# Full-height adapter products in a gated state-space and mixture-of-experts block

## The reference, cut to what matters

```python
xe   = x + w @ muW.T
gate = silu(fused(xe, gW, gqa, gqb, gs, w))
up   =      fused(xe, uW, uqa, uqb, us, w)
out  = fused(gate * up, dW, dqa, dqb, ds, w)

def fused(x, W, qa, qb, scale, w):          # 352 inner features, 8 adapters of rank 8
    a   = einsum('th,krh->tkr', x, qa)      # 64 values a token
    b   = einsum('tkr,khr->tkh', a, qb)
    return x @ W.T + scale * einsum('tkh,tk->th', b, w)
```

## Time and profile before

| what | value |
|---|---|
| median of three runs | 1694.26 us |
| fastest, slowest run | 1688.27, 1695.64 us |
| span of the profiled execution | 1685.8 us |
| PE busy | 1568.4 us, 93% |
| DVE busy | 1155.5 us, 69% |
| POOL busy | 737.8 us, 44% |
| ACT busy | 617.2 us, 37% |
| granted PE clock, mean | 0.977 |

### The profile page before, as it was taken

One profiled execution on the slowest core, in us unless ns is written; L12 is line 12 of the kernel. 1 busy time (PEld: TensorE's weight loads), 2 busy tenths in 40 slices (PEclk: granted clock), 3 DMA queues, 4 the chain that ended last, 5 costly groups with the idle time before them and its releaser, 6 DMA issues.

```text
span 1685.8 us, 19547 instructions
## 1 busy us (share of the span) xinstructions
PE 1568.4 (93%) x6856; PEld 1155.1 (69%) x6856; DVE 1155.5 (69%) x1634; ACT 617.2 (37%) x971; POOL 737.8 (44%) x537
## 2 busy tenths in 40 slices
PE   3787799798888999999999999999999999999999
PEld 2343377566666677777777777777777777777776
DVE  5798964788999867487888755778888553333333
ACT  5545443444454434443343244333433321111111
POOL 4488510489898801077777301376786000000000
PEclk8799999899999999999999999999999999999999
DMA  7688627688787664765667445587665456566552
GB/s 251 215 285 315 254 80 253 201 290 297 270 289 286 253 255 172 248 228 205 232 238 258 152 161 196 202 275 257 238 208 180 175 200 210 184 222 222 195 181 85
DMA packets 111473, 375.87 MB, mean 223 GB/s; under 512 B 20176, under 2 KB 45776, under 8 KB 94864
## 3 DMA queue, kind: packets, MB, share of 16 engines
q1 hardware_dynamic: 101904, 340.81, 57.8%
q10 hardware_dynamic: 9472, 33.82, 5.8%
HBM read 304.33 MB, written 70.25 MB: 222 GB/s over the span
## 4 chain that ended last, share of the span: by engine, by line
PE 63%; DVE 18%; issue 5%; ACT 5%; POOL 4%; DMA 3%; SPq 0%; ACTq 0%; DVEq 0%; POOLq 0%
PE b_g L735 14%; PE b_u L735 14%; PE b_u L826 7%; DVE ring L1493 4%; PE b_g L826 3%; PE b_q L781 3%; PE b_q L826 3%; PE b_g L799 2%; DVE ring L1499 2%; PE b_g L766 2%; DVE tt L1467 2%; POOL ring L1392 2%; PE b_g L759 1%; POOL yx L1401 1%; DVE z L1467 1%
## 5 line engine op out<-in xcount | busy, mean ns | idle before, releaser
L1392 POOL TENSOR_TENSOR ring<-du,rep 128x512 f32<-128x512 f32 x256 | 344.5, 1349 | 151.4 <-DVE du L1571 91.9
L735 PE MATMUL b_g<-xnb,gm 128*128 128x512 f32 (+1 forms) x1440 | 356.2, 396 | 0.9 <-DVE xnb L1470 0.9
L735 PE MATMUL b_u<-xnb,gm 128*128 128x512 f32 (+1 forms) x1440 | 349.1, 391 | 0.0
L1493 DVE TENSOR_TENSOR_SCAN ring<-b_a,ring 128x512 f32<-128x512 f32 x256 | 310.8, 1214 | 15.7 <-ACT b_a L964 8.4
L1401 POOL TENSOR_TENSOR yx<-yx,ring 128x512 f32<-128x512 f32 x192 | 261.8, 1364 | 130.4 <-DVE ring L1499 129.9
L735 PEld LDWEIGHTS b_g<-xnb,gm 128*128 128x128 f32 (+1 forms) x1440 | 252.1, 179 | 89.1 <-issue 24.6
L735 PEld LDWEIGHTS b_u<-xnb,gm 128*128 128x128 f32 (+1 forms) x1440 | 257.1, 179 | 71.1
L1467 DVE SCALAR_TENSOR_TENSOR tt<-tt,b_g 128x512 f32<-128x512 f32 (+1 forms) x120 | 82.1, 684 | 222.7 <-ACT tt L964 222.5
L964 ACT ACTIVATE b_a<-delta,a_neg 128x512 f32<-128x512 f32 x256 | 173.6, 681 | 113.9 <-DVE ring L1493 113.9
L964 ACT ACTIVATE tt<-b_g 128x512 f32<-128x512 f32 (+1 forms) x120 | 71.1, 593 | 316.7 <-PE b_u L766 286.3
L826 PE MATMUL b_u<-dwt,hhl 128*128 128x512 f32 (+1 forms) x720 | 185.4, 394 | 0.0
(11 more groups left out here) (254 smaller groups left out, 2120.2 us busy)
## 6 DMA issues: line engine op xcount, KB each, us to landing
gm<-scr_gm SPq DMA_DIRECT2D x64, 1024.0 KB, 6.8
dwt<-scr_dw SPq DMA_DIRECT2D x32, 1536.0 KB, 6.8
rep<-bc_d ACTq DMA_DIRECT2D x64, 512.0 KB, 5.8
gm<-scr_gm SPq DMA_DIRECT2D x32, 768.0 KB, 4.4
dqt<-scr_dq SPq DMA_DIRECT2D x25, 896.0 KB, 9.1
scr_gm<-gm SPq DMA_DIRECT2D x20, 1024.0 KB, 7.5
scr_dw<-dwt SPq DMA_DIRECT2D x10, 1536.0 KB, 6.2
qat<-scr_qa SPq DMA_DIRECT2D x25, 512.0 KB, 10.2
```

Of the source, the lines that this page charges most:

```text
L735: i = mm(out_b[0:IW[m], :], w, v, start=(n == 0), stop=(n == 11 and not is_routed(s)))
L1392: v.tensor_tensor(ring[:, T % NRING], du[:, T % 4, :], rep[:, N % NREP, 0], ALU.mult).then_inc(pool_dbu, 1)
L1493: v.tensor_tensor_scan(w, ba[T % 2][:], w, 0.0, ALU.mult, ALU.add).then_inc(dve_scan, 1)
```

## The change

The two kinds of adapter operands are put into the two halves of one tile. `qbx` replaces `qbt`, with four slices: in 0 the `gate` hi weights in both halves, in 1 the `up` hi weights in both halves, in 2 the `gate` lo weights above the mask weights of `gate`, in 3 the mask weights of `up` above the lo weights of `up`. `awt` has `aw` to match: `a_g` holds `aw` hi and `aw` lo of `gate`, `aw_g` holds `aw` hi and the soft weights. One matmul with 128 rows is then hi*hi + hi*lo, and a second one is lo*hi plus the mask product. A chunk's adapters are four matmuls with 128 rows in place of four pairs with 64.

```diff
-                g = gqt[r % 2]
-                for j, out_b in ((0, bg[m]), (1, bu[m])):
-                    rows = slice(j * HALF, (j + 1) * HALF)
-                    mm(out_b[0:IW[m], :], g[rows, cols], ws[rows, r % 2], start=False, stop=False)
-                if m == 0:
+                    pe.wait_ge(dma_gq, 32 * (r + 1))
...
-                for k, (hl_, v) in enumerate(((0, aw_h), (0, aw_l), (1, aw_h))):
-                    for j, out_b in ((0, bg[m]), (1, bu[m])):
-                        rows = slice(j * HALF, (j + 1) * HALF)
-                        i = mm(out_b[0:IW[m], :], qbt[rows, hl_, cols], v[rows, :], start=False, stop=(k == 2))
+                for out_b, w, v in ((bg[m], 0, a_g), (bg[m], 2, aw_g[r % 2]), (bu[m], 1, a_u), (bu[m], 3, aw_u[r % 2])):
+                    i = mm(out_b[0:IW[m], :], qbx[:, w, cols], v, start=False, stop=(w >= 2))
```

The operands have to be in both halves, so ACT and DVE write them there. In each routed body:

```diff
@@ def aw_hi (ACT)
-                rounded(aw_h, aw[:]).then_inc(act_aw, 1)
+                k = r % 2
+                for rows, g_ in ((slice(0, HALF), 0), (slice(HALF, P), 1)):
+                    rounded(awt[rows, g_:g_ + 3 + 2 * k:2 + 2 * k],
+                            aw[rows].unsqueeze(1).broadcast_to([HALF, 2, L])).then_inc(act_aw, 1)
@@ def aw_low (DVE)
-                dve.wait_ge(act_aw, rho(s) + 1)
-                lo(aw_l, aw[:], aw_h).then_inc(dve_awl, 1)
+                dve.wait_ge(act_aw, 2 * (rho(s) + 1))
+                lo(awt[HALF:P, 0], aw[0:HALF], awt[0:HALF, 0])
+                lo(awt[0:HALF, 1], aw[HALF:P], awt[HALF:P, 1]).then_inc(dve_awl, 1)
```

In batch 0, where the weights are split in place:

```diff
@@ def hi (ACT)
+                if kind == "qb":
+                    rounded(qbx[0:HALF, 0], src[0:HALF, 0:I])
+                    rounded(qbx[HALF:P, 1], src[HALF:P, 0:I])
+                    rounded(qbx[HALF:P, 0], src[0:HALF, 0:I])
+                    rounded(qbx[0:HALF, 1], src[HALF:P, 0:I]).then_inc(act_hi[slot_of[k]], 1)
+                    return
@@ def lo_piece (DVE)
+                if kind == "qb":
+                    src = raw[slot_of[k]]
+                    lo(qbx[0:HALF, 2], src[0:HALF, 0:I], qbx[0:HALF, 0])
+                    lo(qbx[HALF:P, 3], src[HALF:P, 0:I], qbx[HALF:P, 1]).then_inc(lo_done[slot_of[k]], 1)
+                    return
```

```diff
+            def gqa_load(s):
+                r = rho(s)
+                need(sp, pe_qa, r)
+                sp.wait_ge(dma_gqs, 16 * NF)
+                sp.dma_start(gqa[:].bitcast(F32), scr_gq[r % NF][:, I:GQ]).then_inc(dma_gqa, 16)
             def gq_load(s):
-                if r >= 2:
-                    sp.wait_ge(pe_gu, IC * (body_of(r - 2) + 1))
-                sp.wait_ge(dma_gqs, 16 * NF)
-                sp.dma_start(gqt[r % 2][:].bitcast(F32), scr_gq[r % NF]).then_inc(dma_gq[r % 2], 16)
+                if r >= 1:
+                    sp.wait_ge(pe_gu, IC * (body_of(r - 1) + 1))
+                sp.dma_start(qbx[HALF:P, 2].bitcast(F32), scr_gq[r % NF][HALF:P, 0:I]).then_inc(dma_gq, 16)
+                sp.dma_start(qbx[0:HALF, 3].bitcast(F32), scr_gq[r % NF][0:HALF, 0:I]).then_inc(dma_gq, 16)
...
                 elif i < NX - 1:
                     w_load(s + 1)
+                    gqa_load(s + 1)
+                    next_pieces(s + 1, ("qa", "gm0", "gm1", "gm2"))
                     gq_load(s + 1)
-                    next_pieces(s + 1, ("qa", "gm0", "gm1", "gm2", "qb"))
+                    next_pieces(s + 1, ("qb",))
```

```diff
-            sp.dma_start(cs[:], cst).then_inc(dma_cst, 16)
-            sp.dma_start(inv_i[:], inv.partition_broadcast(NE)).then_inc(dma_cst, 16)
+            sp.dma_start(cs[:, 0:C_GW], cst[:, 0:C_GW]).then_inc(dma_cst, 16)
+            sp.dma_start(cs[:, C_GW:C_GW + 3], cst[:, C_GX:C_ALL]).then_inc(dma_cst, 16)
+            sp.dma_start(gw, cst[:, C_GW:C_GX].rearrange("p (c n) -> p c n", c=HC)).then_inc(dma_cst, 16)
+            sp.dma_start(inv_i, inv.partition_broadcast(NE)).then_inc(dma_cst, 16)
```

More of the change, by code:

```diff
@@ L210, in gated_ssm_moe @@
         dma_x, dma_mu, dma_mq, act_z0 = (sem(n) for n in ("dma_x", "dma_mu", "dma_mq", "act_z0"))
-        dma_stg, dma_gq, dma_wr, dma_ws = (
-            [sem(n + str(k)) for k in range(2)] for n in ("dma_stg", "dma_gq", "dma_wr", "dma_ws"))
+        dma_stg, dma_wr, dma_ws = ([sem(n + str(k)) for k in range(2)] for n in ("dma_stg", "dma_wr", "dma_ws"))
+        dma_gq, dma_gqa = sem("dma_gq"), sem("dma_gqa")
         dma_s0 = [sem("dma_s0_%d" % k) for k in range(4)]
@@ L320, in ready @@
             if from_scratch(s):
-                eng.wait_ge(dma_t[kind], 16 * loads(kind, s))
+                eng.wait_ge(dma_t[kind], loaded(kind) * loads(kind, s))
             elif s == 0:
@@ L408, in load @@
                 free(sp, kind, s)
-                sp.wait_ge(dma_st[kind], 16 * stored_before(kind, s))
+                sp.wait_ge(dma_st[kind], stored(kind) * stored_before(kind, s))
+                if kind == "qb":
+                    at = scr[kind][w_index(s)]
+                    both = at[:, 0:I].rearrange("(j p) i -> p j i", j=2)
+                    for rows in (slice(0, HALF), slice(HALF, P)):
+                        sp.dma_start(qbx[rows, 0:2].bitcast(F32), both).then_inc(dma_t[kind], 16)
+                    sp.dma_start(qbx[0:HALF, 2].bitcast(F32), at[0:HALF, I:2 * I]).then_inc(dma_t[kind], 16)
+                    sp.dma_start(qbx[HALF:P, 3].bitcast(F32), at[HALF:P, I:2 * I]).then_inc(dma_t[kind], 16)
+                    return
                 sp.dma_start(tile_of[kind][:].bitcast(F32).rearrange("p a n -> p (a n)"), scr[kind][w_index(s)]
@@ L444, in w_load @@
                 wsrc = ws_d[e * NK:(e + 1) * NK].rearrange("k r l -> (k r) l")
-                for h in range(2):
-                    sp.dma_start(ws[h * HALF:(h + 1) * HALF, k].bitcast(F32), wsrc).then_inc(dma_ws[k], 16)
+                sp.dma_start(aw_g[k][HALF:P].bitcast(F32), wsrc).then_inc(dma_ws[k], 16)
+                sp.dma_start(aw_u[k][0:HALF].bitcast(F32), wsrc).then_inc(dma_ws[k], 16)
                 for h in range(2):
@@ L576, in _ @@
                     w_load(s + 1)
-                    next_pieces(s + 1, ("gm2", "qb"))
+                    next_pieces(s + 1, ("gm2",))
+                    gq_load(s + 1)
+                    next_pieces(s + 1, ("qb",))
                     next_pieces(s + 1, ("dq",))
```

98 lines of the change are left out of this document (57 added, 41 removed).

## The result

The changed kernel takes 1723.43 us (median of four runs, 1722.56 to 1728.09) beside 1693.73 for the kernel before in the same session: ratio 1.0193, 95% interval 1.0169 to 1.0217. The forecast was 1687 with a range of 1672 to 1700; sign and range were both wrong. The profiled execution spans 1720.8 us against 1685.8, 35 us more.

What follows compares the result with a forecast made beforehand. PE was taken to bound batch 3 and most bodies of batches 1 and 2, DVE batch 0. Terms -10.2 - 9.4 + 11.4 + 0.8 = -7.4 us took 1694.3 to 1687; own range 1681 to 1693, all runs 1672 to 1700.

Steps and rivals of the forecast that it cites:

- the price of the added subtractions: On DVE, `aw_low` becomes two operations, each as long as the one of 0.68 us.
- The delay to `daw_s`: On DVE, `daw_first` and all behind it come 1.18 us later; bounds 0.6 and 2.2.
- its other term, 0.50 of waiting for ACT: DVE waits 0.50 us more before `aw_low`, because ACT's `aw_hi` becomes two operations, 2.1 us in place of 0.63.
- The same fault in qb: Batch 0's second qb subtraction on DVE costs 0.5 us, plus 0.2 of waiting for ACT; 1.6 at most.
- Batch 0: DVE sets the pace; six of seven bodies pay 1.9 us each for both splits: +11.4 us, bounds +3 and +28.
- PE's gain is worth nothing there: In batch 0, where DVE is last, the time PE saves without pairs does not shorten the bodies.
- Batches 1 and 2: PE's gain less DVE's delays comes to -4.7 us a batch, -9.4 for two; bounds -7.05 and about -2.
- Three bodies were to wait for `daw_s`: In batches 1 and 2, bodies e = 0, 3 and 4 lose 0.48 us each through PE's wait, +1.4 a batch.
- Batch 3: PE is the bound in all eight bodies; dropping the pairs saves 1.28 us a body, -10.2 us in all.
- Loads and the start: Five more DMAs a routed body cost nothing; two more issues ahead of the first data cost +0.8 us, bounds 0 and 2.
- Rival C: Added DVE subtractions collide with POOL: batch 0 +32, batches 1 and 2 -4.7, sum +18, 1712 us; chance 0.10.

Runs made afterwards that it cites:

- qb_one: The changed kernel with batch 0's qb weights in one rounding and one subtraction, as before the change; 1707.58 us beside 1690.61 for the kernel before.
- both_one: The changed kernel with the adapter inputs and batch 0's qb weights each in one rounding and one subtraction; 1674.02 us beside 1690.71 for the kernel before.
- aw_one: The changed kernel with the adapter inputs in one 128x512 rounding and one 128x512 subtraction; 1685.87 us beside 1690.61 for the kernel before.
- best: The changed kernel with 64-row pairs in seven batch 0 bodies; elsewhere `aw` in PSUM (e = 1 to 7), four roundings; 1675.13 us beside 1690.71 before.
- aw_psum: The changed kernel with the adapter input of bodies e = 1 to 7 in PSUM instead of SBUF; 1702.52 us beside 1690.32 for the kernel before.

## Why the prediction was wrong

**The step that failed** is the price of the added subtractions: "`aw_low` becomes two operations with the same 512 values a partition, each as long as the one of 0.68". They took 1.16 us each in batch 0 and 1.24 in batches 1 and 2; only in batch 3, where GpSimd has nothing to do, did they take 0.69. The delay to `daw_s` was 3.14 us and not 1.18 (batch 2, e = 3; its other term, 0.50 of waiting for ACT, was right). With `aw` in PSUM the same step costs 1.34: it was worked out rightly for subtractions that GpSimd doesn't hold up.

**The same fault in qb**: "the second costs 0.5 at least", because DVE "has just got through the wait that makes the first one long". It is the other way round. DVE waits 0.85 to 2.0 us for ACT's four roundings and starts 0.1 to 0.5 us before the end of the GpSimd operation in progress, so the first takes 0.52 to 0.89; by then the next GpSimd operation has started, and the second takes 1.51 to 2.07. A body of batch 0 pays 8.5 / 7 = 1.2 more on DVE and (9.4 - 1.4) / 7 = 1.1 more of waiting for ACT, 2.4 in all where 0.5 + 0.2 = 0.7 were forecast; `qb_one` gives 17.2 / 7 = 2.5 back.

**Batch 0**: forecast +11.4, measured +30.3, the two faults above (`both_one`, without the two splits, has -0.3). That PE's gain is worth nothing there was right (-1.3 with PE's side alone).

**Batches 1 and 2**: forecast -4.7 each, measured +6.7 and +6.9. Three bodies were to wait for `daw_s`; with 3.1 us of delay all of e = 0 to 6 did:

```profile
L864 PE MATMUL b_u<-dqt,daw_s 128*128 128x512 f32 x32 | 14.8, 463 | 16.2 <-DVE daw_s L1506 16.2
```

That is 16.2 us in the 16 bodies, where the kernel before has none. The waits are not the whole of the loss. Batch 1 of `aw_one`, with as many matmuls of the same shapes and without these waits, in the columns of the first windows:

```profile
709.35:993.35 284.00, 277.65 (x1221) 219.74 (x1219) 228.56 (x317) 109.62 (x174) 171.99 (x128) 1.00 0.69 228
```

The changed kernel's batch 1 is 12.7 us longer, and 283.11 - 277.65 = 5.5 of these are longer work of PE, not waiting. Some 3.2 of the 5.5 are in e = 3 and 4, whose granted clock is 0.96: 36.75 and 36.81 us busy, where 35.19 is the time at 1.00 (e = 3 in batch 2, e = 4 in `best`). Where the rest lies was not followed up. The last section shows one such stretch, right behind a wait for `daw_s`.

With `best` (from `aw` to `daw_s` 6.16 us in batch 2, e = 3, 0.94 more than before) the two batches come to -4.7 each, the forecast's sum, and nearly body by body: e = 1, 2, 5 and 6 gain 1.1 to 1.2 each, e = 3 and 4 lose 0.4, e = 7 gains 0.9; e = 0, which was to lose 0.48, gains 0.1.

**Batch 3**: forecast -10.2, measured -9.1; the mechanism was right. A chunk keeps 0.02 to 0.07 us around the adapters that the forecast didn't have, and a body is 34.36 and not 34.2.

**Loads and the start**: nothing, as forecast for the loads (`both_one`); the 0.8 us at the start can't be seen among starts that differ by almost 8 us.

**Rival C** was the right one, with 0.10. Its batch 0 (+32) was nearly measured, with some luck in the parts: a body was to pay 2.5 for `aw` and 2.05 for qb, and the edits that take these away give back 16.1 and 17.2 us, 2.3 and 2.5 in each of seven bodies; in qb a part of that is waiting for ACT, which C had at 0.2. Its batches 1 and 2 (-4.7 in all, not +13.6) were too mild, because it priced POOL's operation but not the chain behind it. It was set back by "`aw_low` took 0.68 us in batch 0 with POOL running, the same length as without contention". The reading was wrong: when that subtraction started, at 410.05, no GpSimd operation was in progress. The next one came 0.16 us later:

```profile
410.21 1.48 POOL L1401 TENSOR_TENSOR yx<-yx,ring 128x512 f32<-128x512 f32 x1 [0.34 <-DVE ring L1499]
```

So the row shows who was first, not that there was no contest. The row that would have told it is GpSimd's: 1.48 here, and in batch 2, e = 3, 1.68 for a sum that started 0.15 us behind, where 1.30 is usual. And `aw_hi`, which the same prediction made 1.5 us longer, was what took the start away.

## What to carry to other kernels

Before an unhindered duration is taken for a second operation of its kind, look at the other engine's operation at the same time: if that one is longer than elsewhere, the first was only ahead, and a wait of half a microsecond or one more operation behind it pays the full price. An operand in PSUM took DVE out of that contest (683 to 694 ns in `aw_psum`). And a gain on PE is to be priced together with the work that lays its operands out, on the engine that is last in that stage.

## What was not expected of the hardware

A start 0.05 to 0.16 us earlier decided which engine paid, 0.4 to 0.5 us for GpSimd's sum in batch 2 and up to 1 us for DVE's subtraction. As the forecast had it, a subtraction of 64x512 takes DVE as long as one of 128x512 (686 and 692 ns in batch 3), so a split by partitions doubles its cost even without GpSimd. And one of PE's waits cost more than its length. In batch 1 PE waits 2.54 us for `daw_s` at the end of e = 3; with its next work the granted clock is 0.50 (1.2 GHz) for 2 us and 0.66 in the mean of the next 2, then 1.00 again. (Columns as in the first windows.)

```profile
868.00:870.00 2.00, 0.13 (x1) 0.13 (x2) 2.00 (x4) 1.44 (x4) 0.77 (x1) 0.99 0.00 0
870.00:872.00 2.00, 2.00 (x5) 1.62 (x6) 2.00 (x3) 1.15 (x2) 1.92 (x2) 0.50 0.00 0
872.00:874.00 2.00, 2.00 (x7) 1.53 (x7) 1.95 (x4) 0.00 (x0) 1.86 (x3) 0.66 0.76 256
```

The wait of 2.55 us at the same place of batch 2 left the clock at 1.00. The eight products behind the wait took 3.52 us in batch 1 and 1.95 in batch 2, and the same body took 40.25 us in one and 38.67 in the other. So two bodies with the same work can differ by 1.6 us here. Why the one wait was followed by a lower clock and the other not, no run shows.
